# One block from mixing to the second projection, a new order in the first normalisation and at the first expert tile

## What is computed

```python
def _gat_layer(x, src, dst, W, a_src, a_dst, bias, concat):
    h = (x @ W).reshape(N, H, C)
    e = leaky_relu(al_s[src] + al_d[dst], 0.2)
    m = segment_max(e, dst);  ex = exp(e - m[dst])
    alpha = ex / (segment_sum(ex, dst)[dst] + 1e-16)
    return segment_sum(h[src] * alpha, dst) + bias
...
phi_q, phi_k = exp(q @ rf.T - |q|^2/2), exp(k @ rf.T - |k|^2/2)
attn = (phi_q @ (phi_k.T @ v)) / max(phi_q @ sum(phi_k), 1e-6);  mix = attn @ proj_w.T + proj_b
...
xn = layernorm(x)
x = x + gat2(elu(gat1(xn))) + mix(xn)
x = x + experts(layernorm(x))        # 4 of 32 experts a row, gelu(x W1 + b1) W2 + b2
```

## Time and profile before

| | |
|---|---|
| three runs | 2076.1, 2077.42, 2069.36 us (median 2076.1) |
| profiled execution | 2073.2 us, of which the profile's span is 2071.3 us |
| mean granted clock of PE, as a share of full speed | 0.981 |
| PE busy | 1986.8 us (96%) |
| DVE busy | 1167.3 us (56%) |
| ACT busy | 447.5 us (22%) |
| POOL busy | 185.0 us (9%) |

### The profile page before, as it was taken

How to read it: one execution, slowest core, us unless ns; L and a number is a source line. 1 busy time by engine, 2 the same in 40 slices (tenths; PEclk the granted TensorE clock), 3 DMA queues, 4 the chain that set the end, 5 groups by cost and what they waited for, 6 DMA issues and landing times. The chain is left out here.

```text
span 2071.3 us, 32352 instructions
## 1 busy us (share of the span) xinstructions
PE 1986.8 (96%) x9933; PEld 1467.1 (71%) x9934; DVE 1167.3 (56%) x2548; ACT 447.5 (22%) x822; POOL 185.0 (9%) x181
## 2 busy tenths in 40 slices
PE   5999899998999999999999999999989999999998
PEld 3666666666648887888888755556646777777876
DVE  6666436662566654888888642266863334343343
ACT  3222221222002321222222200013321222122222
POOL 0000000000000000000000000010002323233232
PEclk9999999999999999999999999999987999999999
DMA  8000220002644442732424234544126888899654
GB/s 262 18 17 20 93 108 17 17 19 75 219 144 149 151 128 73 221 124 86 139 91 137 68 146 155 182 125 157 49 75 227 247 270 258 228 286 281 177 137 84
DMA packets 81191, 282.78 MB, mean 137 GB/s; under 512 B 11689, under 2 KB 32225, under 8 KB 71490
## 3 DMA queue, kind: packets, MB, share of 16 engines
q1 hardware_dynamic: 59138, 211.02, 30.5%
q0 software_dynamic: 14848, 56.18, 11.3%
q10 hardware_dynamic: 7104, 14.26, 2.0%
HBM read 217.43 MB, written 63.99 MB: 136 GB/s over the span
## 5 line engine op out<-in xcount | busy, mean ns | idle before, releaser
L1402 PE MATMUL gat_Z<-h_head,first_rest 125*125 125x256 f32 (+1 forms) x1600 | 354.4, 380 | 3.9 <-DVEq L1302 3.9
L1402 PEld LDWEIGHTS gat_Z<-h_head,first_rest 125*125 125x125 f32 x1600 | 297.1, 188 | 49.7 <-issue 4.2
L777 PE MATMUL mix_G<-mix_w,xnT 128*125 128x384 f32 x720 | 246.3, 493 | 3.3 <-PEq L387 2.0
L777 PEld LDWEIGHTS mix_G<-mix_w,xnT 128*125 128x125 f32 x720 | 134.2, 191 | 89.4 <-issue 8.1
L2423 DVE TENSOR_SCALAR ex_idS<-ex_ids 128x1 int32 x52 | 8.0, 153 | 211.4 <-DMA out_rows<-ex_y,ex_idS 211.4
L2510 PE MATMUL ex_PH<-ex_xT,w_and_experts 128*128 128x128 f32 x936 | 113.4, 281 | 1.8 <-issue 0.9
L2510 PE MATMUL ex_PH<-ex_xT,ex_w 128*128 128x128 f32 x936 | 110.9, 277 | 0.5 <-issue 0.2
L2510 PEld LDWEIGHTS ex_PH<-ex_xT,w_and_experts 128*128 128x128 f32 x936 | 108.8, 195 | 2.8 <-issue 2.8
L2520 PE MATMUL ex_PY<-w_and_experts,ex_hT 128*128 128x384 f32 x312 | 107.5, 494 | 0.7 <-ACT ex_hT L2457 0.5
L2520 PE MATMUL ex_PY<-ex_w,ex_hT 128*128 128x384 f32 x312 | 107.3, 494 | 0.8 <-ACT ex_hT L2457 0.6
L2510 PEld LDWEIGHTS ex_PH<-ex_xT,ex_w 128*128 128x128 f32 x936 | 106.5, 192 | 0.7 <-issue 0.7
(11 more groups left out here) (400 smaller groups left out, 3096.2 us busy)
## 6 DMA issues: line engine op xcount, KB each, us to landing
w_and_experts<-in_L_ffn_W SPq DMA_DIRECT2D x32, 1152.0 KB, 8.9
ex_w<-in_L_ffn_W SPq DMA_DIRECT2D x32, 1152.0 KB, 8.5
first_wide<-c_dram SPq DMA_DIRECT2D x40, 546.9 KB
h1T_dram<-gat_oT ACTq DMA_DIRECT2D x40, 250.0 KB, 2.0
mix_w<-in_L_mix_qkv_w SPq DMA_DIRECT2D x6, 1152.0 KB, 12.8
ct_dram<-mix_count_out SPq DMA_DIRECT2D x40, 157.0 KB, 2.1
mix_w_slice<-in_L_gnn_W SPq DMA_DIRECT2D x6, 1024.0 KB, 12.3
proj_w2s<-in_L_gnn_W SPq DMA_DIRECT2D x4, 1536.0 KB, 9.2
```

Source lines behind the costliest of these rows:

```text
L777: last = pe.matmul(G[c][:], xnT[:, k, t * P:(t + 1) * P], w[:, k, c, :], start=(k == 0), stop=(k == KD - 1))
L1402: last = pe.matmul(Z[b][j][:], wt[b][:, s, :], h[hd][0:P, s, j * HC:(j + 1) * HC + j], start=(s == 0), stop=(s == NT - 1))
```

## The change

- From `mix_half_phase(0)` to `gat2_project_phase` there is one block; the PSUM banks become eight shared ones (`bank`), handed on by semaphores. Seven block ends go: before and after either numerator (three of them between the halves and the numerators, one between the second numerator and the projection), after the projection, after the first layer with its clearing of semaphores, and after `gat1`. The ends after the norm, after the second projection and after the route stay. Waits on counters take their place; the semaphores are cleared by POOL at the start of its `gat1` part and at the route's start.
- `first(0)` of the second projection's products moves ahead of the last `turn` of `gat1` (`SecondStart.first_product`), its T1, S and A (`first_sums`) ahead of DVE's last `normalise`. T1 is then kept in memory of `gat1` and copied by ACT to its old place.
- In the first layer's last pair `weights(0)` stands where `slopes` stood, and `slopes` opens `gat1`; the wait for the bias row moves from the beginning of DVE's `gat1` part to the first `normalise`.
- In the norm the scale of the first group stands after the fourth tile's statistics instead of after the seventh's, the copies to `xnT` stand between the statistics, the copies of the edge keys go from DVE to the beginning of ACT's work, and the window rows with POOL's reduction go to the beginning of the mix.
- In the expert phase `turn_x(0)` stands between the units of bias for tiles 7 and 8 and those for tile 9; `indices(1)` on DVE stands ahead of all bias adds; the last unwatched matmul (L2545) goes.

The diff, cut to what sets the order and the waits:

```diff
-            stats_of(*GROUPS[0])
-            variance(0)
-            stats_of(*GROUPS[1])
-            scale(0)
-            variance(1)
-            stats_of(*GROUPS[2])
-            scale(1)
-            variance(2)
...
+            stats_of(0, 3)
+            variance(0)
+            stats_of(3, 4)
+            scale(0)
+            stats_of(4, 6)
+            copy(0)
+            stats_of(6, 7)
+            variance(1)
+            copy(1)
+            scale(1)
+            copy(2)
...
+            for t in range(5, 8):
...
             copy(8)
+            step(dve.tensor_reduce(rng[:, 1, :], df[:], AX.X, ALU.max))
             copy(9)
...
+            for j, dest in enumerate((keyT, sloT)):
+                act.wait_ge(turned, j + 1)
+                act.activation(dest[:, 0:EROWS].rearrange("k (p g) -> k g p", g=EG),
+                               T[j][:].rearrange("k (g p) -> k g p", g=EG), ACT.Copy).then_inc(copied, 1)
...
+                sp.wait_ge(num, 4 + SUMS)
...
+                    window_rows(step, dve, best, win, c1, rng, row1, row, span_ready)
...
+        def numerators(half):
+            pe.wait_ge(s_evac, PER * NT * (half + 1))
...
+                                  start=True, stop=True).then_inc(feat, 1)
+                pe.wait_ge(kv_copied, 2 * (half + 1))
+                for b in range(2):
...
+            sp.wait_ge(num, 4 + SUMS)
...
+                pe.wait_ge(num_used, 2 + SUMS - (1 if t < NT // 2 else 0))
...
+                    elif t == 1:
+                        pe.wait_ge(num_used, 2 + SUMS)
...
+            sp.wait_ge(wa2_step, 2 * KF)
...
+            pool.wait_ge(projected, 2 * NT)
+            pool.wait_ge(summed, 2 * NT)
...
                 if n == PAIRS - 1:
-                    slopes()
+                    weights(0)
                 dve.wait_ge(c22, n + 1)
...
-                if n == PAIRS - 1:
-                    weights(0)
...
+            pe.wait_ge(summed, 2 * NT)
...
+            sp.wait_ge(p3_done, PAIRS)
             sp.dma_start(brow[:], b1.partition_broadcast(128)).then_inc(b_loaded, 16)
...
+            pool.wait_ge(p3_done, PAIRS)
+            cx.release(done_with)
...
+            step(dve.scalar_tensor_tensor(u, u, SLOPE, u, ALU.mult, ALU.max))
...
-            dve.wait_ge(b_loaded, 16)
...
+                if hd == 0 and t == 0:
+                    dve.wait_ge(b_loaded, 16)
...
+                    if last and t == NT - 1:
+                        second.first_sums(dve)
                     normalise(hd, t)
...
+            pe.wait_ge(m_copied, 3)
+            pe.wait_ge(x_kept, 3 * PAIRS)
+            pe.wait_ge(ones_set, H1)
             aggregate(0, 0)
...
                         aggregate(hd + 1, 0)
+                    else:
+                        second.first_product(pe)
                     turn(hd, t)
...
+            sp.wait_ge(turned1, H1 * NT + 2)
+            sp.wait_ge(t_evac1, H1 * NT + 2)
...
-            dve.wait_ge(ext_ready, 2)
-            dve.wait_ge(w_loaded, 128)
-            dve.tensor_tensor(T1[:], B(0, 1), B(0, 0), ALU.subtract).then_inc(t_ready, 1)
-            row_sums(0)
...
+            act.wait_ge(t_ready, 1)
+            act.wait_ge(done, H1 * NT + 2)
+            act.activation(T1[:], second_start.T1, ACT.Copy).then_inc(t1_kept, 1)
...
+                if n == 0:
+                    pe.wait_ge(t1_kept, 1)
...
-            pe.wait_ge(ext_ready, 2)
-            pe.wait_ge(w_loaded, 128)
+            pe.wait_ge(turned1, H1 * NT + 2)
             for n in range(HT):
-                first(n)
+                if n >= 1:
+                    first(n)
...
+    def first_sums(self, dve):
+        dve.wait_ge(self.ext_ready, 2)
+        dve.wait_ge(self.w_loaded, 128)
+        dve.tensor_tensor(self.T1, self.B(0, 1), self.B(0, 0), ALU.subtract).then_inc(self.t_ready, 1)
+        dve.wait_ge(self.first_loaded, 32)
+        dve.tensor_tensor(self.S, self.A(1, 0), self.A(1, 1), ALU.add).then_inc(self.s1_ready, 1)
+        dve.wait_ge(self.s1_ready, 1)
+        dve.tensor_tensor(self.A(1, 0), self.A(0, 0), self.A(1, 0), ALU.subtract).then_inc(self.s3_ready, 1)
+    def first_product(self, pe):
+        pe.wait_ge(self.ext_ready, 2)
+        pe.wait_ge(self.w_loaded, 128)
+        pe.wait_ge(self.first_loaded, 32)
+        for k in range(self.KH):
+            last = pe.matmul(self.bank[0:P, 0:self.W], self.A(0, 0)[:, k * P:(k + 1) * P], self.B(0, 0)[:, k, :],
+                             start=k == 0, stop=k == self.KH - 1, skip_group_check=True)
+        last.then_inc(self.x_done, 1)
...
+    cx.release(done_with)
...
+        def bias_bank(n, m):
+            return 1 if n == 3 else m
...
-            for n, (members, half) in enumerate(UNITS):
+            def add_bias(n):
+                members, half = UNITS[n]
                 dve.wait_ge(b_done, n + 1)
                 for m, t in enumerate(members):
                     col = x1[:, t, half * 384:(half + 1) * 384]
-                    dve.tensor_tensor(col, PY[m][0:P, :], col, ALU.add).then_inc(b_added, 1)
+                    dve.tensor_tensor(col, PY[bias_bank(n, m)][0:P, :], col, ALU.add).then_inc(b_added, 1)
             indices(1)
+            add_bias(0)
             find(2)
+            add_bias(1)
             turn_x(0)
+            add_bias(2)
+            add_bias(3)
             with dve.Fori(0, end) as i:
...
             def second(n, b):
+                pe.wait_ge(b_added, 6)
...
-                    pe.wait_ge(b_added, (0, 2, 4, 5)[n])
+                    pe.wait_ge(b_added, (0, 2, 4, 4)[n])
...
-            for n in range(len(UNITS)):
-                bias(n)
-            pe.wait_ge(b_added, 6)
-            pe.matmul(PY[1][:], ident[:], b2s[:, 0:384], start=True, stop=True)
+            bias(0)
+            bias(1)
             turn_x(0)
+            bias(2)
+            bias(3)
...
+                bank = [pb(nc, st_b, f"bank{j}", [128, 512])[:] for j in range(8)]
+                block = st_b.enter_context(nc.Block(no_gpsimd_drain=True))
...
-            cx.clear()
```

864 lines of the change are left out of this document (446 added, 418 removed).

## The result

The changed kernel takes 2055.88 us in the median (2054.4 to 2061.12, four runs), the kernel before 2076.72 beside it. The ratio, taken over the single runs and not from the two medians, is 0.9915, with a 95% interval of 0.9893 to 0.9936. It is faster by some 20 us, where 35 were forecast, and its time lies 2 us above the stated range. The profiled execution of the changed kernel is the slowest of its four runs, 2061.12 us with a span of 2059.4; against the 2073.2 of before it shows 12 us of gain, which is what is laid out place by place here.

The account below looks back on a forecast made before the run. PE was busy 96% of the span, so only its idle time and its work at the lower clock could come back. The terms summed to 35.3 us off 2073.2, giving about 2038 us, range 2030 to 2054.

Parts of the forecast that it names:

- The norm: Norm and start of the mix: scaling the first group after fewer tiles' statistics saves 2.5 us, bounds 0.5 and 4.0.
- fall into the 3.89 us in which DVE sat idle: Start of the mix: the fifteen small window-row instructions fit DVE's idle 3.89 us, though they may overrun them.
- The doubt that I took from the Trainium skill: Norm: a table switch may cost 2.66 us, not 1.28; the norm would then give 1.1 instead of 2.5.
- Mix to numerators: Mix's end to the numerators, both halves: each saves 2.0 us of idle time and 1.7 us of clock.
- 1.7 us of clock each: Mix to numerators and numerators to second mix: a 3.4 us half-clock stretch goes at each, saving 1.7 us.
- the low clock runs on: Rival: the mix tail's half clock lasts through the numerators in both halves, +62 us, giving 2103 us; chance 0.03.
- Experts: Experts' start: the warm matmul and waits between bias units go, and clock may return earlier; 5.0 us, bounds 3 and 7.
- the loop is as before: Expert loop: no change, since PE hardly waits there and its weights come by the same queue.
- `gat1` to the second projection: From `gat1` to the second projection: idle time, the meeting and clock save 7.1 us, bounds 4.2 and 7.5.
- Only the idle time comes back: Rival: half-clock stretches are not caused by the meetings, so 13.6 us stay, giving 2051 us; chance 0.22.
- The meetings turn into waits: Rival: half of the meetings' 15.2 us idle time stays as semaphore waits, clock as before, 2057.5 us; chance 0.05.
- The reorderings give nothing: Rival: copies hold the norm and the first gather the expert start, 7.5 us missing, 2045 us; chance 0.10.

Follow-up runs that it names:

- before_expert: The kernel before with only the new order at the experts' start; 2075.75 us, ratio to the kernel before 1.0007.
- before_store: The kernel before with only POOL's wait for the stored bias rows moved to the first scatter; 2075.19 us, ratio 1.001.
- the two mends: Changed kernel plus a spare POOL reduction in the norm and POOL's wait for stored bias rows moved to the first scatter; both together 2043.42 us.

## Why the prediction was wrong

The sign was right, and so was the mechanism between the numerators and the second projection; the size was not: the range ended at 2054 and the time is 2055.88. In the two executions laid out above five of its nine terms held within 0.6 us: numerators to the second mix, to the projection, to the first layer, to `gat1`, and the second projection's start. Three steps failed.

The two executions are not typical of how much each step failed. Four profiles have the kernel before up to the gates (two of its own, `before_expert` and `before_store`), and three have the changed kernel. In their means the first key-value sums come 2.7 us later and not 0.4, the two stages from mix to numerators become 5.7 us shorter and not 1.9 longer, and from the gates to the third product (two profiles before) the loss is 3.7 us. By these means nearly 14 of the 17 us that are missing from the forecast gain up to the loop lie in the norm with the start of the mix (5.2) and at the experts (8.7).

*The norm* (forecast 2.5, measured -0.4). The scale was early as worked out: PE's first turn begins at 16.33 instead of 21.10. The step that failed is the one on the window rows, which "fall into the 3.89 us in which DVE sat idle". I priced DVE's instructions and left out POOL's reduction behind them, which the change moves as well and which took 0.59 us in the trace of before. Its first use costs some 9 to 10 us from POOL's coming to it; in the mix 6.4 us of them lay on DVE's path, before the change none. The Trainium skill names such a cost, in "GPSIMD Engine Reference", section "2.1 Instruction dispatch": the first call of a freshly loaded kernel pays a load of about 6 us, with no instruction for it in the profile. The trace agrees that there is one, but has it longer: 8.6 to 9.5 us in four kernels where nothing else was waited for. The page counts without the wait for the input, and without it the mix has 5.8 to 6.7, because the load runs on under that wait.

The norm's own part was also too large. PE's first turn came 4.8 us earlier, but the first mix product only 1.7 (36.75 instead of 38.43), and over all profiles 1.1 (36.4 in nine with the new order, 37.5 in four without). "ACT then runs its ten tiles as before" did not hold: from the first scaled tile to ACT's last copy it took 17.7 us and takes 20.5, with nine waits of 0.2 to 1.3 us in between, for PE's turns and for DVE, where it had three of 0.8 to 1.7. With the reduction mended the first key-value sums come at 67.3 to 68.3, against 67.0 to 71.5 in the kernels with the old norm, so about 1 us of the 2.5 is left. The doubt that I took from the Trainium skill, "ScalarE: Activation LUTs", section "What ACT_TABLE_LOAD costs", was without effect: ACT's second load ends at 12.35 and ACT then still waits 0.9 us for DVE's variance. The load itself is the 1.28 us of the page; a further drain of 1.38 us would not fit into the 0.9 us behind it, so this trace does not agree with it.

*Mix to numerators* (7.4, measured -1.9). The idle 4 us went as forecast. The step that failed is "1.7 us of clock each": I took the stretches of one execution for a property of the place, which at these two meetings they are not. In the four profiles with block ends a half has 6.8 to 13.7 us at half clock there, and the earlier trace rows shows the shortest; without them it is 3.4 to 13.7. The mean is 3.2 us less of it a half with the change, at most 1.6 us of time and near my term, but the halves of one kernel differ by more than that, so this gain is not shown; in the executions compared it was the reverse. The rival *the low clock runs on* named this place and its mechanism, but with a price for both numerators in full and not for a part of them, and only for the changed kernel. The rule of the Trainium skill in "TensorE: Matmul & The Clock Gate", section "What's actually happening", not to fit a cold count, is borne out for the tails. It is not for the stretches behind the four other meetings: these stood in all four profiles with block ends, and the clock's part of those four terms came back.

*Experts* (5.0, measured -2.5). The first product came 3.5 us earlier behind the gates in this execution, as summed. The failed step is "the loop is as before": I followed the second gather to PE and not POOL past it, to its wait for the stores. The gate of 20 us behind the weights was in the trace of before, hidden since PE reached it within 1.0 us. The prediction named "an expert start with a new wait for the gather" as a sign of being wrong, but gave it no price.

*Route* (0, measured -2.5 here): the stage takes 223.1 us in all four profiles of the old order, and 225.6, 222.0 and 225.6 in three of the changed kernel. Where it is long the low clock began earlier in the route's work, here 205.6 us behind the turn in the second projection instead of 215.6 (some 212 in the other three with block ends). Why is open. No kernel tried it.

*The loop* (0, measured -1.4): it varies by more than that from execution to execution, 462.3 and 467.8 us in the two profiles of the kernel before, with waits for gathers of 4.6 and 13.1 us.

*`gat1` to the second projection* (7.1, measured 7.6) came out right with a wrong price in it. "8 x 0.34 = 2.7 us" counts eight records, but the eight matmuls of `first(0)` are sixteen records and take 5.35 us (L1806). The term did not suffer, since these matmuls have to be done in any case and cover the wait of 2.8 us all the better. The high bounds sum to 40.9 and not to 40.8, which changes nothing.

*The rivals.* The time lies nearest to two of them, and neither is what happened. *Only the idle time comes back* gives 2051, but the stretches behind four meetings did go. *The meetings turn into waits* gives 2057.5, but 13.9 of their 15.2 us of idle time did come back. *The reorderings give nothing* came nearest at both of its places, but not by its own reasons (the norm's copies, the first gather), and it was too mild: it took them at 0, and they cost 0.4 and 2.5 us here. The forecast's own mechanism ran, and POOL's late code and the stores' gate took back some 3 to 5 us each, which the two mends return. Even with both, 2043.42 is 5 us above the forecast.

## What to carry to other kernels

When a change moves an instruction, look at each engine that it hands on to: an instruction that cost 0.6 us under cover cost 7 without it. When something starts earlier, follow every queue to the next wait that does not move with it, and ask by how much it was late before: a gate that is met to the microsecond looks like no gate. A clock stretch read from one execution is a sample: take a second profile before pricing it. Here the stretches behind four meetings came every time, those in the sparse mix tails changed from 3.4 to 13.7 us, and behind a wait of 2.0 to 2.3 us at the first layer one came in two kernels (6.8 and 3.4 us) and none in five other profiles (one wait, four meetings).

## What the runs showed of the hardware

POOL's first reduction over the partitions began 8.6 to 10.7 us after POOL came to it, in nine profiles, on nothing that the profile shows; in the five where it was first used in the mix this was 5.8 to 6.7 us after its input. With the first use in the norm, 28 us earlier, and two memsets in between, it began 0.1 us after its input. The mix tails have 3.4 to 13.7 us at 1.2 GHz in each of the eleven profiles without added work, and ran at 2.4 GHz throughout in the two kernels where nine matmuls filled PE's waits in each: eighteen added matmuls took away the low clock there and did not make the kernel slower.
